# An attention and experts kernel: values products in the turned rows' bank, residual later in VectorE's order, reciprocals' factor on GpSimd, first values placed in two groups

## What is computed

```
x = x + attention(layernorm(x), ctx)      # ctx: 4 x 77 x 384; 16 heads of width 32
      q = n(x) Wq + bq;  k = ctx Wk + bk;  v = ctx Wv + bv
      a = softmax(clip(q k^T / sqrt(32), -1e4, 1e4));  out = (a v) Wo + bo
x = x + experts(layernorm(x))
      weights = softmax over the 2 best of 8 experts; each expert takes 1024 tokens at most, in their order
      out[token] += weight * relu(token W1^T) W2^T
```

## Time and profile before

| what | us |
|---|---|
| median of 3 runs (lowest to highest) | 1450.75 (1443.56 to 1451.49) |
| the profiled execution | 1449.84 |
| its span, first to last instruction | 1448.1 |
| TensorE's matmuls busy | 1293.5 (89%) |
| VectorE busy | 973.5 (67%) |
| ScalarE busy | 778.2 (54%) |
| GpSimd busy | 716.6 (49%) |
| score of tile 0 to that of tile 5 (starts) | 52.69 to 116.02 |
| first and last residual (starts) | 129.31 and 735.28 |
| mean granted TensorE clock | 0.959 |

### The profile page before, as it was taken

How to read it: one execution, slowest core, us unless ns; L and a number is a source line. 1 busy time by engine, 2 the same in 40 slices (tenths; PEclk the granted TensorE clock), 3 DMA queues, 4 the chain that set the end, 5 groups by cost and what they waited for, 6 DMA issues and landing times.

```text
span 1448.1 us, 33140 instructions
## 1 busy us (share of the span) xinstructions
PE 1293.5 (89%) x13650; PEld 741.0 (51%) x13650; DVE 973.5 (67%) x1909; ACT 778.2 (54%) x1272; POOL 716.6 (49%) x720
## 2 busy tenths in 40 slices
PE   6757898989999899987738999999999999999996
PEld 3535675656666666664417444444444444444442
DVE  8587898999989987897875545445554545455421
ACT  4467787867888788977345504234251514334210
POOL 3188788777777778876413333242513223241301
PEclk9878999999999999998858999999999999999998
DMA  7137898968798797898523665755747465654401
GB/s 224 45 84 159 215 243 204 250 174 200 194 224 203 150 206 175 191 209 196 147 54 138 177 166 155 154 169 126 185 110 184 137 155 175 148 145 121 107 15 44
DMA packets 320258, 230.12 MB, mean 159 GB/s; under 512 B 253465, under 2 KB 253849, under 8 KB 320106
## 3 DMA queue, kind: packets, MB, share of 16 engines
q1 hardware_dynamic: 304746, 177.33, 51.2%
q0 software_dynamic: 15360, 50.66, 11.9%
HBM read 120.04 MB, written 50.86 MB: 118 GB/s over the span
## 4 chain that ended last, share of the span: by engine, by line
PE 63%; DVE 14%; POOL 8%; ACT 5%; issue 5%; SPq 2%; DMA 1%; DVEq 0%; POOLq 0%; ACTq 0%
PE ps L1237 23%; PE ps L1223 23%; PE ps L1140 6%; PE ps L1070 4%; POOL sd L549 3%; PE ps L1121 2%; DVE ps L1462 1%; PE ps L1013 1%; POOL qT L531 1%; DVE sm L1491 1%; DVE x L1512 1%; DVE sd L1474 1%; POOL oT L537 1%; POOL ph L555 1%; ACT sd L756 1%
## 5 line engine op out<-in xcount | busy, mean ns | idle before, releaser
L1223 PE MATMUL ps<-xT,w1s 128*128 128x512 f16 (+1 forms) x1632 | 336.2, 368 | 1.9 <-DVE xT L1810 1.5
L1237 PE MATMUL ps<-w2s,hT 128*128 128x512 f16 x1536 | 332.8, 379 | 0.0
L852 ACT ACTIVATE hT<-ps 128x512 f16<-128x512 f32 (+1 forms) x136 | 77.8, 572 | 356.5 <-PE ps L1223 356.5
L1223 PEld LDWEIGHTS ps<-xT,w1s 128*128 128x128 f16 x1632 | 160.7, 99 | 175.3 <-issue 1.9
L1237 PEld LDWEIGHTS ps<-w2s,hT 128*128 128x128 f16 x1536 | 150.3, 98 | 181.3
L1070 PE MATMUL ps<-xnT,wqh 128*128 128x256 f16 x1536 | 197.0, 280 | 26.4 <-ACT partq L743 25.2
L600 POOL DMA_INDIRECT out_dram<-ys,idx x64 | 71.7, 1120 | 278.4 <-DVE ys L1850 273.9
L1140 PE MATMUL ps<-woh,oT 128*128 128x512 f16 x768 | 188.6, 392 | 16.5 <-POOL oT L537 14.0
L549 POOL TENSOR_TENSOR sd<-sd,rr 128x1232 f32<-128x1232 f32 x64 | 143.9, 2249 | 118.9 <-ACT rr L761 118.8
L1840 DVE SCALAR_TENSOR_TENSOR hT<-ps,hT 128x512 f16<-128x512 f32 (+1 forms) x136 | 88.7, 658 | 138.1 <-ACT hT L852 138.0
L1070 PEld LDWEIGHTS ps<-xnT,wqh 128*128 128x128 f16 x1536 | 148.6, 100 | 53.5 <-ACT partq L743 30.1
(11 more groups left out here) (226 smaller groups left out, 1894.7 us busy)
## 6 DMA issues: line engine op xcount, KB each, us to landing
xr<-x SPq DMA_DIRECT2D x64, 256.0 KB, 3.7
xrow_dram<-x SPq DMA_DIRECT2D x64, 256.0 KB, 3.8
out_dram<-x SPq DMA_DIRECT2D x64, 256.0 KB, 4.0
stage<-w1T SPq DMA_DIRECT2D x8, 2048.0 KB, 10.6
stage<-w2T SPq DMA_DIRECT2D x8, 2048.0 KB, 9.3
xt<-x SPq DMA_DIRECT2D x59, 256.0 KB, 3.6
xs<-x SPq DMA_DIRECT2D x56, 256.0 KB, 4.2
wqf<-wq SPq DMA_DIRECT2D x1, 1024.0 KB, 7.3
```

What stands on the lines that cost most here:

```text
L1223: ins = pe.matmul(hb[z][:, 0:wide], w1s[e % 2][:, a, k, ic * P:(ic + 1) * P], xT[:, 4 * b + k, cols], start=(k == 0 and i == 0), stop=(k = ...
L1237: ins = pe.matmul(yb[z][:, :], hT[:, a, k, s * P:(s + 1) * P], w2s[e % 2][:, b, k, :], start=(k == 0 and i == 0), stop=(k == 7 and i == 2))
```

## The change

1. The values products go to bank `bT` (shared now with the turned rows), in the tail too; `bA[0]` is left to the output products. So `pv_mm` waits for `tx_lo` of the turn before it, and the next turn waits for ScalarE's two readings.
2. In VectorE's beat the residual (with `oe_out`) stands behind both sums, the reciprocals and `tx_lo`; `add_slots` stands in front of both sums. In the tail's loop nothing moves.
3. `r_scale` leaves ScalarE; GpSimd multiplies the reciprocals by 1024 directly in front of `p_norm`.
4. At the start the maximum of the values is taken in front of the beats, both all-reduces stand in beat -7, the scale is made in beat -7, and the values' high and low halves in beat -6.
5. Of the 25 placings of batch 0, eight stand in beat -5 and 17 in beat -4 behind the first turn of probabilities; the loads of those beats stand behind them.

The diff:

```diff
--- before.py
+++ after.py
@@ -48,11 +48,11 @@
 
 LOADS = "l_k l_wq l_v l_wo l_wt l_em l_b3 l_w1 l_w2"
 FROM_PE = "early tx q s pv o xm om ew pos inv w1p gT f1 f2"
-FROM_ACT = ("kvf n1 hi kb0 xTh qf low e rs phi of bend pick ex w1hi w2hi xn xhi hhi")
+FROM_ACT = ("kvf n1 hi kb0 xTh qf low e phi of bend pick ex w1hi w2hi xn xhi hhi")
 FROM_DVE = ("v zero amax scale fact bos lo kb1 own embc lns lna seed1 normv raw mx "
             "cl sm r xTl x1 l2s l2a seed2 xe oe elo ewl dd mask pm sx gd put pickv acc up idx w1x w2x w1y w1s w2s w1lo w2lo "
             "xlo hlo y gt gs")
-FROM_POOL = "bor made vz allmax chain normp qlo olo pz pn plo n2p w1r w2r"
+FROM_POOL = "rs bor made vz allmax chain normp qlo olo pz pn plo n2p w1r w2r"
 
 
 class Count:
@@ -442,16 +442,19 @@
             sp.dma_start(bob[:, :], boT).then_inc(S["l_wt"], 16)
 
             for h in range(-7, T):
+                if h == -5:
+                    for k in range(8):
+                        values_place(0, k)
                 p_T(h + 4)
+                if h == -4:
+                    for k in range(8, len(pieces)):
+                        values_place(0, k)
                 if h + 14 >= RT + XT:
                     load_x(h + 14)
                 if h >= 1:
                     load_r(h + 4)
                 for t in stats_at(h + 1):
                     load_s(t)
-                if -5 <= h < -2:
-                    for k in range(9 * (h + 5), 9 * (h + 6)):
-                        values_place(0, k)
                 if h == -2:
                     sp.wait_ge(S["made"], 5)
                     sp.wait_ge(S["bor"], 1)
@@ -545,6 +548,8 @@
                     pool.wait_ge(S["kb1"], 6)
                     pool.wait_ge(S["lo"], 3)
                     pool.memset(ph[:, t, :, KALL:NCH * P], 0.0).then_inc(S["pz"], 1)
+                pool.wait_ge(S["r"], t + 1)
+                pool.tensor_scalar(rr[:, t % 2, :], rr[:, t % 2, :], PSC, None, ALU.mult).then_inc(S["rs"], 1)
                 pool.wait_ge(S["rs"], t + 1)
                 pool.tensor_tensor(heads(t), heads(t), rr[:, t % 2, :].unsqueeze(2).to_broadcast([P, HEADS, NKV]),
                                    ALU.mult).then_inc(S["pn"], 1)
@@ -635,7 +640,6 @@
                 Q, part = divmod(h + 9, 2)
                 if h == -7:
                     all_max(3, 4)
-                if h == -6:
                     all_max(2, 5)
                 if h == -3:
                     bias_rows()
@@ -755,11 +759,6 @@
                 act.wait_ge(S["low"], t + 1)
                 act.activation(sd[:, t % SDB, :], sd[:, t % SDB, :], ACT.Exp, scale=lim[:, 4:5]).then_inc(S["e"], 1)
 
-            def r_scale(t):
-                if 0 <= t < T:
-                    act.wait_ge(S["r"], t + 1)
-                    act.activation(rr[:, t % 2, :], rr[:, t % 2, :], ACT.Copy, scale=PSC).then_inc(S["rs"], 1)
-
             def p_hi(t):
                 if not 0 <= t < T:
                     return
@@ -779,7 +778,7 @@
                 if G >= 2 and half == 0:
                     act.wait_ge(S["o"], TG * (G - 1))
                 act.wait_ge(S["pv"], n + 1)
-                src = bA[1 if 2 * G + half >= TAIL + 2 else 0][:, :]
+                src = bT[:, :]
                 act.copy(o_both(G, 0, half), src)
                 if n >= 2:
                     act.wait_ge(S["olo"], n - 1)
@@ -893,14 +892,13 @@
                 if h in (20, 36, 52):
                     second_exp((h - 20) // 16)
                 s_exp(h + 6)
-                steps(ones, 1)
-                r_scale(h + 5)
-                q_hi(Q, 2 * part)
                 if h == -6:
                     act.wait_ge(S["scale"], 5)
                     act.wait_ge(S["lo"], 1)
                     act.activation(flat3(vsh[0:NKV, 0]), flat3(vf[0:NKV, :, :]), ACT.Copy, scale=sv[0:NKV]
                                    ).then_inc(S["hi"], 1)
+                steps(ones, 1)
+                q_hi(Q, 2 * part)
                 if h == -4:
                     act.wait_ge(S["scale"], 5)
                     act.activation(flat3(woh[:, 0]), flat3(wof[:, :, :]), ACT.Copy, scale=so).then_inc(S["hi"], 1)
@@ -1095,7 +1092,7 @@
                                             tile_position=(DH * j, 0))
                 ins.then_inc(S["s"], 1)
 
-            def pv_mm(G, half, n=0):
+            def pv_mm(G, half):
                 if not 0 <= G < NG:
                     return
                 b = G * TG // TPB
@@ -1104,8 +1101,8 @@
                     pe.wait_ge(S["pT1"], 16 * (G + 1))
                     if G % (TPB // TG) == 0:
                         pe.wait_ge(S[f"vb{b}"], VB)
-                if free[f"A{n}"]:
-                    pe.wait_ge(*free[f"A{n}"])
+                if free["T"]:
+                    pe.wait_ge(*free["T"])
                 for g in (2 * half, 2 * half + 1):
                     cols = slice(GW * (g % 2), GW * (g % 2 + 1))
                     spans = [range(NKV * h // P, (NKV * (h + 1) - 1) // P + 1) for h in range(4 * g, 4 * g + 4)]
@@ -1118,10 +1115,10 @@
                         k = PAIRS.index((g, c))
                         K = min(P, KALL - c * P)
                         strip = slice(DH * j, DH * (j + 1))
-                        ins = pe.matmul(bA[n][strip, cols], vb[0:K, b, a, k, strip], pT[0:K, G % 2, d, c, :],
+                        ins = pe.matmul(bT[strip, cols], vb[0:K, b, a, k, strip], pT[0:K, G % 2, d, c, :],
                                         start=(i == begins[j]), stop=(i == ends[j]), tile_position=(0, DH * j))
                 ins.then_inc(S["pv"], 1)
-                free[f"A{n}"] = S["of"], 2 * G + half + 1
+                free["T"] = S["of"], 2 * G + half + 1
 
             def o_mm(t):
                 if not 0 <= t < T:
@@ -1286,7 +1283,7 @@
             for h in range(TAIL, T):
                 G, half = divmod(h, 2)
                 H = inverted_at(h)
-                pv_mm(G + 1, half, 1)
+                pv_mm(G + 1, half)
                 if half == 1:
                     oe_mm(G)
                 o_mm(h)
@@ -1900,6 +1897,9 @@
             dve.wait_ge(S["l_wo"], 80)
             abs_max(3, flat3(wof[:, :, :])).then_inc(S["amax"], 1)
             tx_lo(3)
+            dve.wait_ge(S["kvf"], 8)
+            dve.tensor_reduce(scr[0:NKV, 2:3], flat3(vf[0:NKV, :, :]), AX_X, ALU.max,
+                              apply_absolute_value=True).then_inc(S["amax"], 1)
             route = iter(())
             weights = iter(())
 
@@ -1913,12 +1913,9 @@
                 if h in (22, 38, 54):
                     route = ranking((h - 22) // 16)
                     steps(route, 1)
-                s_sum(h + 5, 0)
-                residual(h)
-                if h % 2:
-                    oe_out(h // 2)
                 if H:
                     add_slots(H)
+                s_sum(h + 5, 0)
                 s_sum(h + 5, 1)
                 for g in ones_at(h):
                     value(g)
@@ -1927,6 +1924,9 @@
                 steps(route, 4)
                 s_recip(h + 5)
                 tx_lo(h + 11)
+                residual(h)
+                if h % 2:
+                    oe_out(h // 2)
                 ln2_stats(h)
                 ln2_aggr(h)
                 if h % 2 == 0:
@@ -1937,11 +1937,10 @@
                     if h == seed_at(b):
                         steps(norm1(b), 9)
                 if h == -6:
-                    alternate(scale_of(3, 5, 4, 2.0 ** -50), scale_of(2, 4, 5, 2.0 ** -50))
-                if h == -5:
                     dve.wait_ge(S["hi"], 3)
                     dve.scalar_tensor_tensor(flat3(vsh[0:NKV, 1]), flat3(vf[0:NKV, :, :]), sv[0:NKV],
                                              flat3(vsh[0:NKV, 0]), ALU.mult, ALU.subtract).then_inc(S["lo"], 1)
+                if h == -5:
                     expert_outputs()
                 if h == -4:
                     dve.tensor_scalar(co, isv, iso, 1.0 / PSC, ALU.mult, ALU.mult).then_inc(S["fact"], 1)
@@ -1956,9 +1955,7 @@
                     steps(route, 99)
                 score(h + 7)
                 if h == -7:
-                    dve.wait_ge(S["kvf"], 8)
-                    dve.tensor_reduce(scr[0:NKV, 2:3], flat3(vf[0:NKV, :, :]), AX_X, ALU.max,
-                                      apply_absolute_value=True).then_inc(S["amax"], 1)
+                    alternate(scale_of(3, 5, 4, 2.0 ** -50), scale_of(2, 4, 5, 2.0 ** -50))
 
             for h in range(TAIL, T):
                 H = inverted_at(h)
```

## The result

| what | before | after |
|---|---|---|
| median of 20 runs (lowest to highest), us | 1448.8 (1442.81 to 1455.04) | 1452.47 (1448.06 to 1459.16) |
| ratio, 95% interval | | 1.0033 (1.0018 to 1.0048) |
| profiled execution, us (its span) | 1449.84 (1448.1) | 1449.55 (1447.8) |
| score of tile 5 starts, us | 116.02 | 110.94 |
| last residual starts, us | 735.28 | 735.62 |

The change costs 0.33% or 4.8 us (1448.8 x 0.0033; the interval gives 2.6 to 7.0). Forecast was 1435, 15 us faster. The number lies inside the range given (1417 to 1457) and inside the band of 0.5% that was called no change, but the sign and the reasons have to be looked at again. So the traces tell where time was won and lost, and the runs tell how much.

The account below looks back on a forecast made before the run. Attention stage decides: a start-up chain, then TensorE and VectorE nearly full, ScalarE also full from 403 us. Terms -2 - 9 - 3 - 1 = -15 take the profiled 1449.84 us to 1435; range 1417 to 1457.

Parts of the forecast that it names:

- Start-up (-2): Up to 116 us: one pair of GpSimd switches goes, the queue gives much of it back; 2 us faster.
- ends -11 and +3: Up to 116 us, limits of the estimate: whole lead kept, 11 us faster; only the late load, 3 us slower.
- The wait of "about 10 us": Before 116 us: VectorE would wait about 10 us for tile 15's load, issued near 97 us.
- Beats to tile 27 (-9): From 120 to 403 us: VectorE's 14.2 us of residual waits go, 0.2 us a beat comes back; 9 us faster.
- from tile 28 (-3): From 403 to 655 us: fewer waits for queries' bank and residual, against later turned rows in even beats; 3 us faster.
- The bank swap by itself has no term of its own: In the beats: both output and values products freed from waits, counted inside the beats' estimate, with no separate size.
- The sign named: On TensorE: waits of 0.3 us or more in front of most values products would show the forecast wrong.
- The shared bank costs more: In the beats: values products wait for VectorE to read the turned rows; 0.45 us a beat gives 1460 us; chance 0.16.
- More of it holds: Whole kernel: start-up keeps its lead, beats fall to the busier of TensorE and VectorE; -31, 1419 us; chance 0.12.
- Held by something else: Whole kernel: DMA, or GpSimd and VectorE slowing each other, limits the gain; -5, 1445 us; chance 0.18.
- Tail (-1): From 655 to 740 us: ScalarE's 8.7 us of waits for reciprocals lie mostly beside TensorE's turns; 1 us faster.
- Factor (0): In the beats: GpSimd's multiplication of the reciprocals, 18 us in all, costs nothing against its 116.7 us of waiting.

Follow-up runs that it names:

- the pair: Values products moved to the turned rows' bank and VectorE's order changed together, on the kernel before, nothing else changed: 1462.99 us, ratio 1.0086.

## Why the prediction was wrong, point by point

**Start-up (-2): right in mechanism and side, too small.** One pair of switches went. The first normalisation came at 69.97 (forecast 72) and the first turn at 76.77 (78.7). The load for tile 15 was issued at 94.97 (97.3): 1.9 us from the earlier turn, 0.4 from 17 placings at 14.37 / 17 = 0.845 in place of 0.87. It landed 3.2 us later, where I had taken the median of 4.2, so VectorE went on at 98.14 (101.5). Those 3.4 us are nearly all of what was missing: score of tile 5 at 110.94, against a forecast of 115.0 less 1 for ScalarE's copies. The turn was early mainly because the first score came 0.2 us later (52.87 against 52.69) and not the 2.3 us that I had given the maximum. Alone the part is worth 6.2 us (3.9 to 8.7), inside the ends -11 and +3. The wait of "about 10 us" was 12.55. The trace shows 7.74 us in front of the first subtraction behind the all-reduces, so the way back does cost, and it was paid once in place of twice. The Trainium skill ("GPSIMD Engine Reference", section 2.1, Instruction dispatch) names a cost for the first call alone; by it the start-up would have come out at +5, and the runs decide against that.

**Beats to tile 27 (-9) and from tile 28 (-3): this is the step that failed.** The half on VectorE came as forecast: no residual wait is left, TensorE's waits for the queries' bank went too, VectorE's waits for the copy are short (5.4 us up to 403). In the trace of the change they brought 0 and +7 us. What failed is the sentence "The bank swap by itself has no term of its own". I had checked whether VectorE's low half would be late by more than before, and priced that at 0.1 + 0.1 us on VectorE. I had not asked what TensorE has left to do at that moment. Its answer is nothing: the next thing in its strict order is the product that needs the bank. The sign named was 0.3 us in front of most values products; the trace has 49.3 us in 47 waits, 1.05 us each.

The gain was mis-sized too. The -9 counted VectorE's 14.2 us in front of the residual as time. They went, but they were not time: the kernel with start and factor but without the pair (0.9951) has 32.6 us of that wait from 120 to 655 us, the change with the values products late (0.9947, same chip) has none, and the two are level.

**Its size.** For beats and tail I had forecast -13; the pair alone measured +12.5 (8.4 to 16.4). The difference of 25.5 us over 55 beats is 0.46 us in each. The loss itself, 12.5 us, is 0.23 us a beat, a quarter of the new wait (49.3 / 55 = 0.90), since other waits of TensorE went: from 120 to 655 us of the change it was idle for 10 us more in all. The rival "The shared bank costs more" named the mechanism and the price, 0.45 us a beat, and its point of decision, 0.27. It had a chance of 0.16. Its time was 1460 with a start-up of -2; with the real one of -6 it is 1456, and the runs say 1452.5 (as a ratio of the 1450.75 shown then, 1455.5). What spoke against it, "up to 300 us the copy ends before VectorE is free", was the wrong test. It compares the copy with VectorE, while the wait is TensorE's and ends with VectorE's low half, behind both sums. In the beat shown above copy and VectorE fit each other within 0.02 us, and TensorE still waited 1.09.

**The other rivals.** "More of it holds" and "Held by something else" did not come. DMA was busy 0.95 of the time from 150 to 300 us, as before, and VectorE's waits for a load came to 1.5 us in three places from 120 to 403 us. Locks between GpSimd and VectorE were not isolated; the factor on GpSimd, which would have brought them nearer, changed nothing.

**Tail (-1).** The last score starts 1.3 us late and the last residual 0.3 us, so the tail gave back 1 us in this pair of traces, as forecast. No run isolates it, and 1 us is within the spread of executions: that may be luck.

**Factor (0).** Right: 0.9994.

**The loss from tile 36 on.** In the change, 6.4 us of lead turned into 1.9 us of delay. The pair's own trace loses 0.17 us a beat from tile 6 to tile 36 and 0.39 from there to tile 60. From tile 36 on ranking and slots' inversions fill TensorE's and VectorE's beats, and there is less spare time to take up a wait. That this is the reason is my reading; the one part that I took back there, the slots' sum, made no difference.

## What to carry to other kernels

When a tile moves to another bank, write down for each of the two users who the last reader is, where that reader stands in its engine's order, and what the waiting engine still has to do before it needs the bank. Look also at what stands behind the wait: a wait also holds up what other engines need from behind it. Here one line, the scores ahead of the values products, was worth 12 us, though TensorE still waited 33.2 us for the bank. And two edits can each be a clear loss (2.0% and 2.9%) and together a smaller one (0.9%), so take a change apart by pairs as well as by single parts.
In a strict queue, put the short load that someone is waiting for ahead of a row of transfers that nobody needs yet.
